# Attention block on one core: the fp32r high and low parts become fp16 pairs

## The chip, the cores and the metric

One Trainium2 chip, one core of it. The time is device microseconds (us) of one execution, the median of several; lower is better. The trace is one profiled execution. Engines: TensorE (PE, with its weight loads PEld), VectorE (DVE), ScalarE (ACT), GpSimd (POOL), SyncE (SP, which here only issues DMAs).

## The reference

Self-attention over 16 images of 32 x 32 positions (1024 tokens) with 512 channels, 8 heads of 64, all in fp32, with a residual:

```python
x = ft.reshape(B, N, C)                          # (16, 1024, 512)
qkv = x @ w_qkv + b_qkv                          # (16, 1024, 1536)
q, k, v = jnp.split(qkv.reshape(B, N, N_HEADS, 3 * D_HEAD), 3, axis=-1)
attn = jnp.einsum('bxhd,byhd->bxyh', q, k) * SCALE
attn = jax.nn.softmax(attn, axis=2)
res = jnp.einsum('bxyh,byhd->bxhd', attn, v).reshape(B, N, N_HEADS * D_HEAD)
res = res @ w_out + b_out + x
```

## The kernel before

fp32 accuracy is had from narrow matmuls: each operand is split into a high and a low part, and a product a·b is summed as hi·hi + hi·lo + lo·hi (`three_terms`). Before, x, both weights, q, k and the attention output are held as fp32r pairs (4 bytes an element); the probabilities (`p_hi`, `p_lo`) and v (`v_parts`) are fp16 pairs already.

The work is cut into 64 *steps* per image (`STEPS`), 1024 steps in all. Four steps make a *unit*: one head, 512 queries, all 1024 keys, two key tiles of 128 per step. Two units are a head, sixteen an image. In a step:

- TensorE makes the scores of the next step, for each of two key tiles one matmul with k_lo over k_hi against q_hi (L628) and one with the shift and k_hi against the row maxima and q_lo (L630), 512 columns each, into one of three PSUM banks in turn (`score_bank`);
- it makes one to three *row-max* matmuls for the next unit (L592, 512 columns, two ring banks): scores with the queries on the partitions, of which VectorE takes the maximum (L841). Once a unit the four maxima are transposed (L600) and VectorE writes them, negated, as rows of `q_shift` (L851), so that a matmul subtracts them;
- ScalarE reads each score tile twice with Exp, to fp32 (`p_full`, L740) and to fp16 (`p_hi`, L741); GpSimd (six steps in eight, L489) or VectorE (two, L860) subtracts the two into `p_lo`;
- TensorE multiplies the probabilities of the step before with v (L653 to L658): 22 fp16 matmuls of 64, 65 or 129 columns, with the probabilities stationary. The document calls these 22 the PV matmuls.

Between the two score tiles of a step stand the *fills*, work of other stages in pieces of 12 matmuls or parts of 12 (L573): the q/k projection of the next heads (`qk`, 512 columns), v (`v`, 256 columns), the output projection (`project`, 512 columns). Before a `project`, four fp32 transposes (L582) turn a token tile of the attention output. `fills_of_slot`, `ring_early`, `ring_late` and the tables above them fix by hand at which step each piece stands; every engine runs its list in order and waits on semaphores.

The parts are split as follows: ScalarE writes the high part by a copy that rounds (`x_hi` L693, `weights_hi` L698, `qk_hi` L723 and L725, `transposed_hi` L714); the low part is source minus high part, by VectorE for the weights (L785), the first image's x (L797), q and k (L824, L827) and the attention output (L808), and by GpSimd for x of later images (L483). After `qk_hi`, SP issues two DMAs inside SBUF that copy the upper half of q_hi and of k_hi to the other partitions (L427, L430).

Of the kernel before, what the change touches and what calls it, by code (L numbers as in the profile page):

```python
# [6 lines left out]
P = 128  # L7
# [6 lines left out]
PROB_BIAS = 8 * math.log(2)  # L14
QKV = 3 * DIM
# [212 lines left out]
def attention_block(nc: bass.Bass, x, xT, w_qkv, b_qkv, w_out, b_out, out):  # L228
    f32, f32r, f16 = mybir.dt.float32, mybir.dt.float32r, mybir.dt.float16
# [5 lines left out]
    with ExitStack() as ctx:  # L235
# [5 lines left out]

        wqkv_hi = sb("wqkv_hi", [P, CH_TILES, HEADS * QKV], f32r)
        wqkv_lo = sb("wqkv_lo", [P, CH_TILES, HEADS * QKV], f32r)
        wout_hi = sb("wout_hi", [P, CH_TILES, CH], f32r)
        wout_lo = sb("wout_lo", [P, CH_TILES, CH], f32r)
        xT_hi = sb("xT_hi", [P, CH_TILES, TOKENS], f32r)
        xT_lo = sb("xT_lo", [P, CH_TILES, TOKENS], f32r)
        oT_hi = sb("oT_hi", [P, O_SLOTS, CH_TILES, P], f32r)
        oT_lo = sb("oT_lo", [P, O_SLOTS, CH_TILES, P], f32r)
# [12 lines left out]
        qk_bias = sb("qk_bias", [P, HEADS], f32)  # L262
        v_bias = sb("v_bias", [P, CH_TILES], f32)
# [22 lines left out]
        consts_in = sem("consts_in")  # L286
        w_hi_done = sem("w_hi_done")
# [94 lines left out]
        def _(sp):  # L382
# [91 lines left out]
        def _(pool):  # L474
# [214 lines left out]
        def _(act):  # L689
# [20 lines left out]
            act.wait_ge(consts_in, 64)  # L710

# [5 lines left out]
            def qk_hi(b, w):  # L717
# [17 lines left out]
            def exp_tile(g, n):  # L735
                if n == 0:
# [209 lines left out]
```

## Time and profile before

| | |
|---|---|
| time, median of 3 runs | 3830.77 us (3830.4 to 3831.52) |
| span of the profiled execution | 3830.3 us |
| TensorE, matmuls | 99% of the span |
| TensorE, weight loads | 80% |
| ScalarE | 79% |
| VectorE | 71% |
| GpSimd | 52% |

The span runs from the first to the last instruction of the one profiled execution; it lies inside the range of the timed runs, so about 0.5 us stands between it and the median. A matmul's end is modelled, so TensorE's 99% is not a measure of how full it is: the distance from one matmul's start to the next one's is. On ScalarE, VectorE and GpSimd, rows that follow each other overlap at their ends a little, too.

### The profile page before, as it was taken

How to read it: one execution, taken by the hardware profiler on the slowest of the kernel's cores; microseconds unless marked ns; L12 is line 12 of the kernel's file. 1: busy time of each engine (PE TensorE's matmuls, PEld its weight loads, DVE VectorE, ACT ScalarE, POOL GpSimd, SP SyncE). 2: the span in 40 equal slices, each digit the busy share in tenths (PEclk: the TensorE clock that was granted, in tenths of full speed). 3: DMA queues.
4: the chain of work that ended last, by engine and by line, in shares of the span. 5: the costliest groups of instructions: out<-in, count | busy, mean ns of one | idle time of the engine just before them, and what ended most of it. 6: DMA issues, size and time to landing. Idle time of an engine off the chain costs nothing.

```text
span 3830.3 us, 93450 instructions
## 1 busy us (share of the span) xinstructions
PE 3776.0 (99%) x37132; PEld 3081.0 (80%) x37132; DVE 2715.5 (71%) x4643; ACT 3044.9 (79%) x5141; POOL 1983.5 (52%) x1022
## 2 busy tenths in 40 slices
PE   7999999999999999999999999999999999999998
PEld 5878888887888888888888888878888788888886
DVE  6777767777676776777767677776776767767775
ACT  5887878878787887878878788787887878878786
POOL 2464644556445464454645546455454544646444
PEclk9999999999999999999999999999999999999999
DMA  3011111212102121021211211112011111111111
GB/s 94 21 54 45 54 47 26 59 40 56 48 23 67 35 56 48 21 73 29 56 48 34 66 26 54 48 40 65 23 54 48 51 51 26 54 48 43 51 25 54
DMA packets 100709, 178.26 MB, mean 47 GB/s; under 512 B 16192, under 2 KB 16192, under 8 KB 100288
## 3 DMA queue, kind: packets, MB, share of 16 engines
q1 hardware_dynamic: 100288, 172.29, 16.2%
q8 instruction: 307, 5.03, 0.5%
q14 instruction: 114, 0.93, 0.1%
HBM read 71.57 MB, written 33.55 MB: 27 GB/s over the span
## 4 chain that ended last, share of the span: by engine, by line
PE 91%; POOL 2%; issue 2%; DVE 2%; ACT 2%; DMA 0%; SPq 0%; ACTq 0%; DVEq 0%
PE psum L573 35%; PE psum L592 13%; PE psum L628 11%; PE psum L630 11%; PE psum L653 5%; PE psum L655 5%; PE psum L654 4%; PE psum L658 3%; PE psum L657 1%; PE psum L582 1%; POOL xT_lo L483 1%; POOL p_lo L489 1%; PE psum L600 1%; ACT p_hi L741 1%; DVE max_parts L841 0%
## 5 line engine op out<-in xcount | busy, mean ns | idle before, releaser
L489 POOL TENSOR_TENSOR p_lo<-p_full,p_hi 128x1024 f16<-128x1024 f32 x768 | 1647.7, 2145 | 1681.1 <-ACT p_hi L741 1679.8
L841 DVE TENSOR_REDUCE max_parts<-psum 128x1 f32<-128x512 f32 x2048 | 1376.3, 684 | 595.2 <-PE psum L592 594.5
L740 ACT ACTIVATE p_full<-psum,prob_bias 128x512 f32<-128x512 f32 x2048 | 1425.6, 696 | 260.7 <-PE psum L630 246.4
L741 ACT ACTIVATE p_hi<-psum,prob_bias 128x512 f16<-128x512 f32 x2048 | 1422.1, 694 | 0.0
L592 PE MATMUL psum<-k_lo_hi,q_hi_hi 128*128 128x512 f32 x2048 | 854.2, 437 | 12.0 <-DMA q_hi_hi<-q_hi_hi 6.7
L628 PE MATMUL psum<-q_hi_hi,k_lo_hi 128*128 128x512 f32 x2048 | 810.3, 396 | 6.3 <-DVE q_shift L851 3.4
L630 PE MATMUL psum<-q_shift,k_shift 128*128 128x512 f32 x2048 | 805.0, 393 | 0.0
L653 PEld LDWEIGHTS psum<-v_parts,p_hi 128*128 128x128 f16 x6144 | 568.0, 98 | 280.2 <-issue 248.4
L653 PE MATMUL psum<-v_parts,p_hi 128*128 128x65 f16 x6144 | 765.1, 194 | 11.5 <-POOL p_lo L489 11.5
L654 PE MATMUL psum<-v_parts,p_hi 128*128 128x64 f16 x6144 | 756.3, 193 | 0.0
L655 PE MATMUL psum<-v_parts,p_lo 128*128 128x65 f16 x6144 | 752.6, 194 | 0.0
L655 PEld LDWEIGHTS psum<-v_parts,p_lo 128*128 128x128 f16 x6144 | 576.0, 97 | 0.0
L654 PEld LDWEIGHTS psum<-v_parts,p_hi 128*128 128x128 f16 x6144 | 575.3, 97 | 0.2
L592 PEld LDWEIGHTS psum<-k_lo_hi,q_hi_hi 128*128 128x128 f32 x2048 | 384.6, 188 | 81.8 <-issue 23.0
L658 PE MATMUL psum<-v_parts,p_hi 128*128 128x129 f16 x2048 | 447.5, 219 | 0.0
L630 PEld LDWEIGHTS psum<-q_shift,k_shift 128*128 128x128 f32 x2048 | 385.6, 188 | 72.2
L628 PEld LDWEIGHTS psum<-q_hi_hi,k_lo_hi 128*128 128x128 f32 x2048 | 387.8, 189 | 68.5 <-ACT p_hi L741 13.6
L573 PE MATMUL psum<-xT_hi,wqkv_hi 128*128 128x512 f32 x1024 | 408.1, 399 | 14.3 <-DVE xT_lo L797 14.3
L851 DVE SCALAR_TENSOR_TENSOR q_shift<-psum,identity 4x512 fp32r<-4x512 f32 x256 | 173.8, 679 | 343.5 <-PE psum L600 340.9
L573 PE MATMUL psum<-xT_lo,wqkv_hi 128*128 128x512 f32 x1024 | 402.6, 393 | 0.0
L573 PE MATMUL psum<-xT_hi,wqkv_lo 128*128 128x512 f32 x1024 | 401.3, 392 | 0.0
L657 PE MATMUL psum<-v_parts,p_lo 128*128 128x65 f16 x2048 | 393.8, 192 | 0.0
(71 smaller groups left out, 5799.6 us busy)
## 6 DMA issues: line engine op xcount, KB each, us to landing
q_hi_hi<-q_hi_hi SPq DMA_DIRECT2D x256, 128.0 KB, 2.2
k_shift<-k_lo_hi SPq DMA_DIRECT2D x256, 128.0 KB, 2.2
y_tile<-in_x SPq DMA_DIRECT2D x125, 256.0 KB, 2.7
result<-y_tile SPq DMA_DIRECT2D x125, 256.0 KB, 2.0
x_in<-in_xT SPq DMA_DIRECT2D x121, 256.0 KB, 2.9
o_heads<-in_L_conv_w_qkv SPq DMA_DIRECT2D x12, 256.0 KB, 4.5
p_full<-in_xT SPq DMA_DIRECT2D x4, 256.0 KB, 5.1
o_heads<-in_L_conv_w_out SPq DMA_DIRECT2D x4, 256.0 KB, 3.2
```

Source lines behind the costliest of these rows:

```text
L489: nc.gpsimd.tensor_tensor(p_lo[:, g % LO_SLOTS, :, :], p_full[:, g % 2, :, :], p_hi[:, g % HI_SLOTS, :, :], ALU.subtract).then_inc(p_lo_re ...
L573: matmul = nc.tensor.matmul(bank(b, w)[:, 0:width], stationary, moving, start=n == 0, stop=n == TERMS - 1)
L592: nc.tensor.matmul(bank(b, w), q_hi_hi[:, h % 2, q0:q0 + P], k_lo_hi[:, h % 2, k_half * HALF:(k_half + 1) * HALF], start=True, stop=True). ...
L628: nc.tensor.matmul(scores(g, n), k_lo_hi[:, h % 2, keys], q_hi_hi[:, h % 2, cols], start=True, stop=False)
L630: nc.tensor.matmul(scores(g, n), k_shift[:, h % 2, keys], q_shift[:, h % 2, cols], start=False, stop=True).then_inc(scores_ready, 1)
L653: nc.tensor.matmul(pv[:, qt, :], hi, v_hi, start=kt == 0 and qt == 1, stop=False, skip_group_check=True)
L654: nc.tensor.matmul(pv[:, qt, 0:DIM], hi, v_lo, start=False, stop=False, skip_group_check=True)
L655: nc.tensor.matmul(pv[:, qt, :], lo, v_hi, start=False, stop=end, skip_group_check=True)
L658: last = nc.tensor.matmul(pv_first, hi, v_all, start=False, stop=end, skip_group_check=True)
L740: nc.scalar.activation(p_full[:, g % 2, n, :], scores(g, n), ACT.Exp, scale=SCALE, bias=prob_bias[:, :])
L741: nc.scalar.activation(p_hi[:, g % HI_SLOTS, n, :], scores(g, n), ACT.Exp, scale=SCALE, bias=prob_bias[:, :]).then_inc(exp_done, 1)
L841: nc.vector.reduce_max(max_parts[:, u % 2, q_tile, k_half:k_half + 1], bank(b, w), AX.X).then_inc(done["row_max"], 1)
```

## The change

Everything held in fp32r becomes fp16: `wqkv`, `wout`, `xT`, `oT`, `k_lo_hi`, `k_shift`, `q_hi_hi`, `q_shift`. The weights are multiplied by 16 when they are split (`W_SCALE`): q and k then carry a factor of 16, which the scale of Exp takes out, and the two projections in a row one of 256, which `project_add` takes out. The row of ones that carries the shift becomes 4096 and the shift is divided by 4096. The bias of q and k is multiplied by 16 once at the start (one small ScalarE instruction, a semaphore, and one wait on ScalarE and one on VectorE, before the loop). Five VectorE lines that had one operation now have two fused in one instruction (`scalar_tensor_tensor` for `tensor_tensor`); the copies by DMA carry 2 bytes an element.

On each of the five engines the lists of instructions before and after stand in the same order, row against row, with the one added ScalarE instruction at the start as the only difference in number; the loop has the same instructions with the same waits.

The core of the diff (the same edit repeated at other tensors and places is left out):

```diff
+W_SCALE = 16.0
+SHIFT_UNIT = 4096.0
...
-        wqkv_hi = sb("wqkv_hi", [P, CH_TILES, HEADS * QKV], f32r)
+        wqkv_hi = sb("wqkv_hi", [P, CH_TILES, HEADS * QKV], f16)
...
-        xT_hi = sb("xT_hi", [P, CH_TILES, TOKENS], f32r)
+        xT_hi = sb("xT_hi", [P, CH_TILES, TOKENS], f16)
...
-        k_lo_hi = sb("k_lo_hi", [P, 2, TOKENS], f32r)
+        k_lo_hi = sb("k_lo_hi", [P, 2, TOKENS], f16)
...
-                sp.dma_start(q_hi_hi[DIM:P, h % 2, cols].bitcast(f32),
-                             q_hi_hi[0:DIM, h % 2, cols].bitcast(f32)).then_inc(q_hi_hi_ready[half], 16)
+                sp.dma_start(q_hi_hi[DIM:P, h % 2, cols],
+                             q_hi_hi[0:DIM, h % 2, cols]).then_inc(q_hi_hi_ready[half], 16)
...
-                nc.gpsimd.tensor_tensor(lo, x_stage(b, n), hi.bitcast(f32),
+                nc.gpsimd.tensor_tensor(lo, x_stage(b, n), hi,
                                         ALU.subtract).then_inc(x_lo_done, 1)
...
-                    nc.scalar.copy(weight_part(part, c)[0], stage[:, stage_slot(part, c), :]).then_inc(w_hi_done, 1)
+                    nc.scalar.activation(weight_part(part, c)[0], stage[:, stage_slot(part, c), :], ACT.Copy,
+                                         scale=W_SCALE).then_inc(w_hi_done, 1)
...
             act.wait_ge(consts_in, 64)
+            nc.scalar.activation(qk_bias_scaled[:, :], qk_bias[:, :], ACT.Copy, scale=W_SCALE).then_inc(qk_bias_ready, 1)
+            act.wait_ge(qk_bias_ready, 1)
...
-                nc.scalar.activation(p_full[:, g % 2, n, :], scores(g, n), ACT.Exp, scale=SCALE, bias=prob_bias[:, :])
+                nc.scalar.activation(p_full[:, g % 2, n, :], scores(g, n), ACT.Exp, scale=SCALE / (W_SCALE * W_SCALE), bias=prob_bias[:, :])
...
-            nc.vector.memset(k_shift[0:Q_TILES, :, :].bitcast(f32), 1.0).then_inc(fixed_ready, 1)
+            nc.vector.memset(k_shift[0:Q_TILES, :, :], SHIFT_UNIT).then_inc(fixed_ready, 1)
...
-                    nc.vector.tensor_tensor(lo, stage[:, stage_slot(part, c), :], hi.bitcast(f32), ALU.subtract).then_inc(w_lo_done, 1)
+                    nc.vector.scalar_tensor_tensor(lo, stage[:, stage_slot(part, c), :], W_SCALE, hi, ALU.mult,
+                                                   ALU.subtract).then_inc(w_lo_done, 1)
...
-                nc.vector.tensor_tensor(y, bank(b, w), y, ALU.add).then_inc(done["project"], 1)
+                nc.vector.scalar_tensor_tensor(y, bank(b, w), 1 / (W_SCALE * W_SCALE), y, ALU.mult,
+                                               ALU.add).then_inc(done["project"], 1)
```

## Rows read from the trace of the kernel before

**Rows 1.** The page: busy time by engine; the core's span and clock; the chain's shares.
```profile
PE 3776.0 (99%) x37132; PEld 3081.0 (80%) x37132; DVE 2715.5 (71%) x4643; ACT 3044.9 (79%) x5141; POOL 1983.5 (52%) x1022
core 0: 3830.3 us, clock 0.998
PE 91%; POOL 2%; issue 2%; DVE 2%; ACT 2%; DMA 0%; SPq 0%; ACTq 0%; DVEq 0%
```

**Rows 2.** Groups by line and shape: count, then busy us, mean ns of one.
```profile
L628 PE MATMUL psum<-q_hi_hi,k_lo_hi 128*128 128x512 f32 x2048 | 810.3, 396 | 6.3 <-DVE q_shift L851 3.4 <-ACT p_hi L741 0.9
L573 PE MATMUL psum<-xT_hi,wqkv_hi 128*128 128x512 f32 x1024 | 408.1, 399 | 14.3 <-DVE xT_lo L797 14.3
L573 PE MATMUL psum<-wqkv_hi,xT_lo 128*128 128x256 f32 x1024 | 290.3, 283 | 0.0
L573 PE MATMUL psum<-wout_hi,oT_hi 128*128 128x512 f32 x512 | 206.1, 402 | 2.4 <-DVE oT_lo L808 1.6 <-DVE x_in L836 0.8
...
L653 PEld LDWEIGHTS psum<-v_parts,p_hi 128*128 128x128 f16 x6144 | 568.0, 98 | 280.2 <-issue 248.4 <-ACT p_hi L741 29.8
L628 PEld LDWEIGHTS psum<-q_hi_hi,k_lo_hi 128*128 128x128 f32 x2048 | 387.8, 189 | 68.5 <-ACT p_hi L741 13.6 <-DVE q_shift L851 11.8
```

**Rows 3.** Timeline of TensorE (start, length, what), a fill's end and a step.
```profile
1000.37 0.40 PE L573 MATMUL psum<-wout_hi,oT_lo 128*128 128x512 f32 x1
...
1003.36 0.20 PE L653 MATMUL psum<-v_parts,p_hi 128*128 128x65 f16 x1
...
1004.03 0.22 PE L658 MATMUL psum<-v_parts,p_hi 128*128 128x129 f16 x1
```

**Rows 4.** The chain that ended last in order of time: one `v` fill.
```profile
1503.17 1.43 PE psum L573 x12
```

**Rows 5.** A stretch at the start at half clock: busy by engine; timeline.
```profile
31.92:36.83 4.91, 4.91 (x25) 4.91 (x23) 0.69 (x1) 0.37 (x1) 0.00 (x0) 0.50 0.00 0
31.92 0.41 PE L573 MATMUL psum<-wqkv_hi,xT_hi 128*128 128x256 f32 x1
...
36.83 0.36 PE L573 MATMUL psum<-wqkv_hi,xT_lo 128*128 128x256 f32 x1
```

**Rows 6.** Timeline of TensorE where a PV stretch ends.
```profile
1506.29 0.22 PE L658 MATMUL psum<-v_parts,p_hi 128*128 128x129 f16 x1
1506.31 0.48 PE L592 MATMUL psum<-k_lo_hi,q_hi_hi 128*128 128x512 f32 x1
...
1506.86 0.40 PE L630 MATMUL psum<-q_shift,k_shift 128*128 128x512 f32 x1
```

**Rows 7.** One stretch: us, busy PE, PEld, DVE, ACT, POOL, clock; chain's end.
```profile
445.50:459.00 13.50, 12.86 (x132) 9.84 (x129) 10.62 (x18) 13.40 (x24) 10.07 (x6) 1.00 0.41 121
...
456.72 2.10 POOL p_lo L489
458.95 0.19 PE psum L653
```

**Rows 8.** Timelines of VectorE and TensorE where a new head's k is split.
```profile
586.01 0.76 DVE L824 SCALAR_TENSOR_TENSOR k_lo_hi<-psum,qk_bias,k_lo_hi 64x512 fp32r<-64x512 f32 x1
...
586.86 0.47 PE L592 MATMUL psum<-k_lo_hi,q_hi_hi 128*128 128x512 f32 x1
```

**Rows 9.** Timelines of VectorE and TensorE, row maxima with two in a row.
```profile
1509.36 0.69 DVE L841 TENSOR_REDUCE max_parts<-psum 128x1 f32<-128x512 f32 x1 [1.84 <-PE psum L592]
...
1509.87 0.74 PE L592 MATMUL psum<-k_lo_hi,q_hi_hi 128*128 128x512 f32 x2
1510.44 0.39 PE L628 MATMUL psum<-q_hi_hi,k_lo_hi 128*128 128x512 f32 x1
```

**Rows 10.** Groups of ScalarE and GpSimd by line and shape.
```profile
L740 ACT ACTIVATE p_full<-psum,prob_bias 128x512 f32<-128x512 f32 x2048 | 1425.6, 696 | 260.7 <-PE psum L630 246.4 <-POOL p_lo L489 3.2
L741 ACT ACTIVATE p_hi<-psum,prob_bias 128x512 f16<-128x512 f32 x2048 | 1422.1, 694 | 0.0
L489 POOL TENSOR_TENSOR p_lo<-p_full,p_hi 128x1024 f16<-128x1024 f32 x768 | 1647.7, 2145 | 1681.1 <-ACT p_hi L741 1679.8
L483 POOL TENSOR_TENSOR xT_lo<-x_in,xT_hi 128x512 fp32r<-128x512 f32 x120 | 176.5, 1481 | 71.2 <-ACT xT_hi L693 71.2
```

**Rows 11.** Who waited for whom: total us, times, longest.
```profile
PE psum L592 <- DMA q_hi_hi<-q_hi_hi: 6.7, 1, 6.7
```

More of the change, by code:

```diff
@@ L286, in attention_block @@
         consts_in = sem("consts_in")
+        qk_bias_ready = sem("qk_bias_ready")
         w_hi_done = sem("w_hi_done")
@@ L703, in value_bias_hi @@
                 for c in range(CH_TILES):
-                    nc.scalar.activation(bias_hi[:, c, :], zeros, ACT.Identity, bias=v_bias[:, c:c + 1]).then_inc(w_hi_done, 1)
+                    nc.scalar.activation(bias_hi[:, c, :], zero_tile[:, :], ACT.Identity, bias=v_bias[:, c:c + 1]).then_inc(w_hi_done, 1)
             weights_hi(0)
@@ L723, in qk_hi @@
                 nc.scalar.activation(q_hi_hi[0:DIM, h % 2, cols], bank(b, w)[0:DIM, :], ACT.Identity,
-                                     bias=qk_bias[0:DIM, h:h + 1]).then_inc(q_hi_done, 1)
+                                     bias=qk_bias_scaled[0:DIM, h:h + 1]).then_inc(q_hi_done, 1)
                 nc.scalar.activation(k_lo_hi[DIM:P, h % 2, cols], bank(b, w)[DIM:P, :], ACT.Identity,
-                                     bias=qk_bias[DIM:P, h:h + 1]).then_inc(hi_done["qk"], 1)
+                                     bias=qk_bias_scaled[DIM:P, h:h + 1]).then_inc(hi_done["qk"], 1)
             def v_hi(b, w):
@@ L739, in exp_tile @@
                 wait(act, scores_ready, KEYS_PER_STEP * g + n + 1)
-                nc.scalar.activation(p_full[:, g % 2, n, :], scores(g, n), ACT.Exp, scale=SCALE, bias=prob_bias[:, :])
+                nc.scalar.activation(p_full[:, g % 2, n, :], scores(g, n), ACT.Exp, scale=SCALE / (W_SCALE * W_SCALE), bias=prob_bias[:, :])
                 nc.scalar.activation(p_hi[:, g % HI_SLOTS, n, :], scores(g, n), ACT.Exp,
-                                     scale=SCALE, bias=prob_bias[:, :]).then_inc(exp_done, 1)
+                                     scale=SCALE / (W_SCALE * W_SCALE), bias=prob_bias[:, :]).then_inc(exp_done, 1)
             for g, batches in SLOTS:
@@ L796, in _ @@
                 hi, lo = x_part(n)
-                nc.vector.tensor_tensor(lo, x_stage(0, n), hi.bitcast(f32), ALU.subtract).then_inc(first_x_lo_done, 1)
+                nc.vector.tensor_tensor(lo, x_stage(0, n), hi, ALU.subtract).then_inc(first_x_lo_done, 1)
             weights_lo(1)
             dve.wait_ge(consts_in, 64)
+            dve.wait_ge(qk_bias_ready, 1)
             def bias_of_output():
                 dve.wait_ge(bias_product, 1)
-                nc.vector.tensor_tensor(out_bias[:, :], psum[:, PV_BANK, :], out_bias[:, :], ALU.add).then_inc(bias_ready, 1)
+                nc.vector.scalar_tensor_tensor(out_bias[:, :], psum[:, PV_BANK, :], 1 / W_SCALE, out_bias[:, :], ALU.mult,
+                                               ALU.add).then_inc(bias_ready, 1)
             def transposed_lo(b, w):
@@ L823, in qk_lo @@
                 cols = slice(half * HALF, (half + 1) * HALF)
-                nc.vector.scalar_tensor_tensor(k_lo_hi[0:DIM, h % 2, cols], src[DIM:P, :], qk_bias[DIM:P, h:h + 1],
-                                               k_lo_hi[DIM:P, h % 2, cols].bitcast(f32), ALU.add,
+                nc.vector.scalar_tensor_tensor(k_lo_hi[0:DIM, h % 2, cols], src[DIM:P, :], qk_bias_scaled[DIM:P, h:h + 1],
+                                               k_lo_hi[DIM:P, h % 2, cols], ALU.add,
                                                ALU.subtract).then_inc(k_lo_done, 1)
-                nc.vector.scalar_tensor_tensor(q_shift[DIM:P, h % 2, cols], src[0:DIM, :], qk_bias[0:DIM, h:h + 1],
-                                               q_hi_hi[0:DIM, h % 2, cols].bitcast(f32), ALU.add,
+                nc.vector.scalar_tensor_tensor(q_shift[DIM:P, h % 2, cols], src[0:DIM, :], qk_bias_scaled[0:DIM, h:h + 1],
+                                               q_hi_hi[0:DIM, h % 2, cols], ALU.add,
                                                ALU.subtract).then_inc(done["qk"], 1)
@@ L852, in shift_rows @@
                     q_shift[0:Q_TILES, h % 2, half * HALF:(half + 1) * HALF].rearrange("r (t q) -> r t q", q=P),
-                    bank(b, w)[0:Q_TILES, 0:P].rearrange("r (o q) -> r o q", o=1).broadcast_to([Q_TILES, Q_TILES, P]), -1.0,
+                    bank(b, w)[0:Q_TILES, 0:P].rearrange("r (o q) -> r o q", o=1).broadcast_to([Q_TILES, Q_TILES, P]), -1.0 / SHIFT_UNIT,
                     identity[0:Q_TILES, 0:Q_TILES].rearrange("r (t o) -> r t o", o=1).broadcast_to([Q_TILES, Q_TILES, P]),
```

37 lines of the change are left out of this document (19 added, 18 removed).

## The prediction, made before the changed kernel was run

> **What bounds the kernel now.** I read the page first: the chain of work that ended last lies on TensorE for 91% of the span, and the other engines are busy 79%, 71% and 52% [rows 1]. That matmuls are "busy" 99% says little, since their ends are modelled; so the second view is the timeline of TensorE, where I measure from start to start. Three things are to be seen there. First, the 512-column fp32r matmuls follow each other without a gap: from 1000.37 to 1003.36 there are 13 of them, 2.99 us, 230 ns each [rows 3]; the 256-column ones take 1.43 us for 12, 119.2 ns [rows 4]. Second, at full clock (2.4 GHz, granted share 0.998 [rows 1]) 512 and 256 columns at one a cycle are 213.3 and 106.7 ns: 16.7 and 12.5 ns of each matmul are not columns. At the start, where the granted share is 0.50 (1.2 GHz), 23 matmuls of 256 columns take 4.91 us, 213.5 ns each [rows 5], just 256 cycles: there the extra is hidden. Third, the fp16 matmuls of PV: from 1003.36 to 1004.03 there are 21, with 2 x 776 - 129 = 1423 columns, which are 592.9 ns; the rows give 670 ns, so 3.7 ns extra per matmul [rows 3]. The difference between the types that a row shows is the weight load: 98 ns a record for fp16, 189 ns for fp32r [rows 2]. So the kernel is bound by the rate at which TensorE takes matmuls, and the fp32r ones carry an extra that fp16 ones of the same kernel don't.
>
> **The change part by part.** No instruction of the loop is moved, added or taken away; the types change.
>
> *512-column matmuls.* L628, L630 and L592 have 2048 each, the q/k projection 3 x 1024, the output projection 3 x 512 [rows 2] (one row of each kind stands there): 10752. With the fp16 extra each takes 213.3 + 3.7 = 217.0 ns, 13.0 less: 139.8 us. No row shows a 512-column fp16 matmul. Its bounds are the column rate alone (213.3) and the present 230; I take 217.0, because it is the extra of 21 fp16 matmuls with weight loads of the same 128 x 128 shape.
>
> *256-column matmuls.* 3 x 1024 [rows 2]: 119.2 to 106.7 + 3.7 = 110.4, 8.8 less: 27.0 us.
>
> *From PV to fp32r.* From the last PV matmul at 1506.29 to 1506.86, 0.57 us pass for 129 + 512 + 512 columns [rows 6]; by the rates above they would be 57.5 + 230 + 230 = 517.5 ns. So 52.5 ns are lost there: an fp32r load behind short matmuls is not covered. That is 53 ns as 128 columns at 2.4 GHz would be. It stands in three of a unit's four steps (in the fourth the small transpose L600 stands between), 768 times: 40.3 us, gone when all is fp16. The fp32 transposes L582 keep their type; they follow 512-column matmuls, which cover their load, so I add nothing.
>
> Together 207.1 us of TensorE's time. What of it lies on the path? Three places give some back, because TensorE then arrives before something that it already only just meets.
>
> *Once an image.* Between 445.5 and 459.0 ScalarE is busy 13.40 of 13.50 us, and the stretch ends with GpSimd's p_lo at 456.72 + 2.10 and PV at 458.95 [rows 7]: four steps in which x of the next image is split and q/k of a new head are read out. There ScalarE and GpSimd set the pace. TensorE's 132 matmuls are 88 of PV and 44 others; 44 x 13 + 3 x 52.5 ns = 0.73 us are gained for nothing, 15 times: 11 us.
>
> *A new head's k.* L592 at 586.86 starts just as VectorE's L824 ends (586.01 + 0.76) [rows 8]. From the L592 before it TensorE would gain 5 matmuls and one change of type, 0.12 us, and wait instead. There are 128 heads: 15 us at most, none at least; I take 8.
>
> *Two row maxima in a row.* The second L592 starts about 1510.19 (one matmul and a bit before 1510.44), 0.14 us after the reduction that frees its bank (1509.36 + 0.69 = 1510.05) [rows 9]. That is close to a wait; what TensorE gains since the third L592 (2 x 13 + 53 = 79 ns) may be lost in each of 256 units: 0 to 20 us; I take 10.
>
> *ScalarE.* Writing fp16 costs what fp32 costs: 694 against 696 ns [rows 10]. Its 79% would become 83% of the shorter span; L740 alone now idles 260.7 us, 246.4 of them behind TensorE [rows 10], so there is room for 207 us spread over the image.
>
> *GpSimd.* L483 gets the types of L489: fp32 and fp16 in, fp16 out. Half of L489's 2145 ns would be 1073, all of it 2145, against 1481 now [rows 10]. Three stand in each of the 15 stretches: from -18 to +30 us. I take none, the present 1481 being between the two and nearer to the half.
>
> *VectorE* keeps one pass over the same elements; a fused multiply is no second pass: L824 is such an instruction and takes 0.76 us for 512 columns [rows 8] where L841 takes 0.69 [rows 9]. With 128 project_adds at 0.07 us more, beside TensorE's work, this costs nothing. *DMA*: the copies carry half the bytes; the one wait for them is 6.7 us at the start [rows 11]: 0 to 4 us less, taken as none. The added bias instruction stands before the loop, behind the same start: under 1 us.
>
> Sum: 207.1 - 11 - 8 - 10 = 178 us; 3830.3 - 178 = 3652.3, and with the 0.5 us between the span and the median 3653 us.
>
> A page bears on the first term. The Trainium skill, "TensorE: Matmul & The Clock Gate", section "Wait — 56ns, not 53.3ns?", gives a fixed 2.5 ns per warm bf16 matmul, 215.7 ns for 512 columns. By it the two matmul terms would be 154 and 31 us, and the time about 3635; [rows 3] show 3.7 ns for short fp16 matmuls, and none here is 512 wide.
>
> **The rivals.**
>
> *Half of the extra belongs to the columns.* From 256 to 512 columns the fp32r matmul grows by 110.8 ns, 0.433 ns a column, where 2.4 GHz asks for 0.417 [rows 3, 4]. If fp16 keeps these 0.016 ns, it takes 225.2 and 114.5 ns: 10752 x 4.8 + 3072 x 4.7 + 40.3 = 106 us, less 15 for the three places: 3740 us. For it: two widths, one line. Against: at half clock columns cost exactly a cycle [rows 5], and four bytes a column are a trait of fp32r.
>
> *The load is covered anyway.* Behind 512 columns a load has 213 ns, and 53 is enough. Then the extra is not the load's, and only the 768 changes of type gain: 40 - 15 = 25 us, 3805 us. For it: loads fill 80% of the span beside matmuls that fill 99% [rows 1], so most of them lie under matmuls. Against: the extra differs by type. The Trainium skill says so in the same page, section "Step-by-step: what each phase is for", where the next weights load while the present matmul runs, and in "Weight-path perf modes", where the fast load, which fp32 doesn't get, is said to win with a small free dimension; by these rules 512 columns would gain nothing. Against it stand the 230 ns of [rows 3], where 216 would be all.
>
> *fp16 columns are slower.* TensorE's fp16 stream is known here only up to 129 columns. If wide fp16 matmuls paid more per column than fp32r ones, the loop would lengthen: with rows in hundredths, 129 against 65 columns is 60 against 30 ns, 0.47 a column, and 512 columns would be 240 ns; 10752 x 10 - 40 = 67 us, 3897 us. It decides from 234 ns a matmul, where 10752 x 4 eats the 40 us. Against: 21 matmuls average 3.7 ns over the column rate [rows 3].
>
> *Nothing reaches the end*: ScalarE and VectorE take it all back, 3830 us. Against it are ScalarE's 260 us behind TensorE.
>
> **How the numbers follow.** Forecast 0.64, half at the columns 0.20, covered anyway 0.09, slower 0.04, nothing 0.03. The predicted time is the forecast's, 3653. Its own bounds: 207 us and 18 from GpSimd and 4 from the copies, less 11, give 3612; with 46 us given back at the three places and 30 on GpSimd, 3699. The range must reach into the second case: 3615 to 3750 leaves about 0.19 out. A measurement of this kernel can tell about 0.2% from no change (8 us). Faster 0.64 + 0.20 + 0.09 = 0.93, same 0.03, slower 0.04.
>
> **What would show it.** Right: runs of 512-column matmuls at 217 ns from start to start and of 256 at 110; 129 + 512 + 512 columns behind PV in 0.49 us; the once-an-image stretch still about 13.4 us with ScalarE full; weight loads of L628 at 98 ns; ScalarE about 83%. Wrong: 225 ns or 230 ns for a 512-column matmul; or 217 with TensorE idle before L592, L628 and L653 for more than 50 us in sum, and VectorE or ScalarE as what ended it; or GpSimd's L483 over 2 us.

## The result and the profile after

The changed kernel takes 3603.12 us (median of 4, 3602.55 to 3604.41); the kernel before, beside it, 3830.61. The ratio is 0.9406, 95% interval 0.9392 to 0.9419: 227.5 us faster. The prediction of 3653 had the sign right and the gain some 50 us too small; the measured time lies below its range (3615 to 3750).

The page of the kernel after, busy time by engine and the shares of the chain (as in [rows 1]):

```profile
PE 3527.6 (98%) x37132; PEld 2155.3 (60%) x37132; DVE 2689.1 (75%) x4643; ACT 3015.9 (84%) x5142; POOL 1949.6 (54%) x1022
...
PE 84%; ACT 5%; POOL 4%; issue 3%; DVE 2%; DMA 0%; SPq 0%; ACTq 0%; DVEq 0%
```

TensorE still carries the chain, for 84% where it was 91%; the busy shares of ScalarE and VectorE have risen by five and four points, to 84% and 75%. The weight loads have lost 926 us of busy time. The span is 3600.7 us, 229.6 less than before; the steps below are booked against that.

Groups by line and shape (as in [rows 2] and [rows 10]; L577, L632, L634, L747 and L487 are L573, L628, L630, L740 and L483 of before; mean ns of one stands before the second bar):

```profile
L632 PE MATMUL psum<-q_hi_hi,k_lo_hi 128*128 128x512 f16 x2048 | 777.1, 379 | 18.2 <-ACT p_hi L748 10.3 <-DVE q_shift L862 6.7
L634 PEld LDWEIGHTS psum<-q_shift,k_shift 128*128 128x128 f16 x2048 | 200.3, 98 | 199.8
L747 ACT ACTIVATE p_full<-psum,prob_bias 128x512 f32<-128x512 f32 x2048 | 1430.5, 698 | 176.8 <-PE psum L634 152.3 <-POOL p_lo L493 3.4
L487 POOL TENSOR_TENSOR xT_lo<-x_in,xT_hi 128x512 f16<-128x512 f32 x120 | 158.6, 1331 | 54.6 <-ACT xT_hi L697 54.6
```

The load of a score matmul is 98 ns, where it was 189. ScalarE's Exp is unchanged (698 ns). GpSimd's x split is 150 ns shorter on average.

Timeline of TensorE, a whole fill, the next scores and a PV stretch (as in [rows 3]), and then the end of a PV stretch (as in [rows 6]; L596 is L592 of before, L657 to L662 are PV):

```profile
939.57 0.38 PE L577 MATMUL psum<-wout_hi,oT_hi 128*128 128x512 f16 x1
...
942.80 0.19 PE L657 MATMUL psum<-v_parts,p_hi 128*128 128x65 f16 x1
...
943.47 0.22 PE L662 MATMUL psum<-v_parts,p_hi 128*128 128x129 f16 x1
...
1415.56 0.22 PE L662 MATMUL psum<-v_parts,p_hi 128*128 128x129 f16 x1
1415.61 0.38 PE L596 MATMUL psum<-k_lo_hi,q_hi_hi 128*128 128x512 f16 x1
...
1416.04 0.38 PE L634 MATMUL psum<-q_shift,k_shift 128*128 128x512 f16 x1
```

From 939.57 to 942.80 there are 15 wide matmuls: 215.3 ns each by the rows. Over all 512-column fills the starts in the two traces give 215.8 ns, where 230.1 stood before. The 21 of PV take 0.67 us, as before. From the last PV matmul to the third wide one's start 0.48 us pass (1415.56 to 1416.04), where 0.57 did [rows 6]. A `v` fill in the chain (as in [rows 4]) takes 109.2 ns a matmul where it took 119.2:

```profile
432.18 1.31 PE psum L577 x12
```

By stage (starts of TensorE's records): the first PV comes 4.5 us earlier (63.3 to 58.8), 2.0 of it because the one wait for `q_hi_hi`'s copy is 4.7 us for 6.7 [rows 11]; the first image becomes 12.8 us shorter, each of the next fourteen 14.13 (235.86 to 221.72), the last 11.7, and the tail behind the last PV 2.7. Together 229.5: the gain is spread evenly, an image at a time. About half of the tail's gain is not the change's own: before, seven wide matmuls there stand 427 ns apart at a granted clock of 0.50 (1.2 GHz), 1.4 us more than at 230, and after, the granted clock of the tail is 1.00. The view of that stretch before, as in [rows 5]:

```profile
3812.40:3815.39 2.99, 2.99 (x9) 2.32 (x7) 0.00 (x0) 0.00 (x0) 0.00 (x0) 0.50 0.00 0
```

### The profile page after: what moved, and what is told of

The parts are those of the page before. It is cut to its first block, busy times and chain, and to the rows that moved or that the text cites. A ratio compares the mean times of both kernels' runs of the same rounds, so it can differ in the third digit from the quotient of the medians.

```text
span 3600.7 us, 93452 instructions
## 1 busy us (share of the span) xinstructions
PE 3527.6 (98%) x37132; PEld 2155.3 (60%) x37132; DVE 2689.1 (75%) x4643; ACT 3015.9 (84%) x5142; POOL 1949.6 (54%) x1022
## 4 chain that ended last, share of the span: by engine, by line
PE 84%; ACT 5%; POOL 4%; issue 3%; DVE 2%; DMA 0%; SPq 0%; ACTq 0%; DVEq 0%
PE psum L577 33%; PE psum L596 11%; PE psum L632 10%; PE psum L634 10%; PE psum L659 4%; PE psum L657 4%; PE psum L658 4%; POOL p_lo L493 3%; PE psum L662 3%; ACT p_full L747 2%; ACT p_hi L748 2%; PE psum L586 2%; PE psum L661 1%; POOL xT_lo L487 1%; PE psum L604 1%
## 5 line engine op out<-in xcount | busy, mean ns | idle before, releaser
L747 ACT ACTIVATE p_full<-psum,prob_bias 128x512 f32<-128x512 f32 x2048 | 1430.5, 698 | 176.8 <-PE psum L634 152.3
L632 PE MATMUL psum<-q_hi_hi,k_lo_hi 128*128 128x512 f16 x2048 | 777.1, 379 | 18.2 <-ACT p_hi L748 10.3
L634 PE MATMUL psum<-q_shift,k_shift 128*128 128x512 f16 x2048 | 776.2, 379 | 0.0
L657 PE MATMUL psum<-v_parts,p_hi 128*128 128x65 f16 x6144 | 754.3, 192 | 12.0 <-POOL p_lo L493 12.0
L596 PE MATMUL psum<-k_lo_hi,q_hi_hi 128*128 128x512 f16 x2048 | 743.9, 380 | 16.8 <-DMA q_hi_hi<-q_hi_hi 4.7
L657 PEld LDWEIGHTS psum<-v_parts,p_hi 128*128 128x128 f16 x6144 | 585.8, 98 | 136.1 <-issue 22.8
L662 PE MATMUL psum<-v_parts,p_hi 128*128 128x129 f16 x2048 | 448.1, 219 | 0.0
L862 DVE SCALAR_TENSOR_TENSOR q_shift<-psum,identity 4x512 f16<-4x512 f32 x256 | 173.7, 679 | 315.2 <-PE psum L604 311.2
L577 PE MATMUL psum<-xT_hi,wqkv_hi 128*128 128x512 f16 x1024 | 388.8, 380 | 15.0 <-DVE xT_lo L805 15.0
L577 PE MATMUL psum<-xT_lo,wqkv_hi 128*128 128x512 f16 x1024 | 388.6, 380 | 0.0
L577 PE MATMUL psum<-xT_hi,wqkv_lo 128*128 128x512 f16 x1024 | 388.6, 380 | 0.0
L871 DVE TENSOR_TENSOR p_lo<-p_full,p_hi 128x1024 f16<-128x1024 f32 x256 | 318.2, 1243 | 37.5 <-ACT p_hi L748 33.5
L634 PEld LDWEIGHTS psum<-q_shift,k_shift 128*128 128x128 f16 x2048 | 200.3, 98 | 199.8
L596 PEld LDWEIGHTS psum<-k_lo_hi,q_hi_hi 128*128 128x128 f16 x2048 | 198.2, 97 | 186.3 <-DVE max_parts L852 76.5
```

What stands on the lines that cost most here:

```text
L577: matmul = nc.tensor.matmul(bank(b, w)[:, 0:width], stationary, moving, start=n == 0, stop=n == TERMS - 1)
L596: nc.tensor.matmul(bank(b, w), q_hi_hi[:, h % 2, q0:q0 + P], k_lo_hi[:, h % 2, k_half * HALF:(k_half + 1) * HALF], start=True, stop=True). ...
L632: nc.tensor.matmul(scores(g, n), k_lo_hi[:, h % 2, keys], q_hi_hi[:, h % 2, cols], start=True, stop=False)
L634: nc.tensor.matmul(scores(g, n), k_shift[:, h % 2, keys], q_shift[:, h % 2, cols], start=False, stop=True).then_inc(scores_ready, 1)
L657: nc.tensor.matmul(pv[:, qt, :], hi, v_hi, start=kt == 0 and qt == 1, stop=False, skip_group_check=True)
L662: last = nc.tensor.matmul(pv_first, hi, v_all, start=False, stop=end, skip_group_check=True)
```

## Experiments: do the parts add up?

Three kernels hold one part in fp16 pairs and leave the others in fp32r; the fourth is the kernel after with one part left in fp32r. All four keep the scale factors and the fused instructions of the kernel after. The types that differ, for the first three against the kernel before:

```diff
 # e1_qk_only (types against before)
-        q_hi_hi = sb("q_hi_hi", [P, 2, TOKENS], f32r)
+        q_hi_hi = sb("q_hi_hi", [P, 2, TOKENS], f16)      # also k_lo_hi, k_shift, q_shift
 # e2_xw_only (types against before)
-        xT_hi = sb("xT_hi", [P, CH_TILES, TOKENS], f32r)
+        xT_hi = sb("xT_hi", [P, CH_TILES, TOKENS], f16)   # also xT_lo, wqkv_hi, wqkv_lo
 # e3_o_only (types against before)
-        oT_hi = sb("oT_hi", [P, O_SLOTS, CH_TILES, P], f32r)
+        oT_hi = sb("oT_hi", [P, O_SLOTS, CH_TILES, P], f16)   # also oT_lo, wout_hi, wout_lo
 # e10_all_but_o (from after)
-        oT_hi = sb("oT_hi", [P, O_SLOTS, CH_TILES, P], f16)
+        oT_hi = sb("oT_hi", [P, O_SLOTS, CH_TILES, P], f32r)  # also oT_lo, wout_hi, wout_lo
```

> Only q and k (k_lo_hi, k_shift, q_hi_hi, q_shift) are fp16 pairs; x, the weights and the attention output stay fp32r. Sum of parts: 6144 matmuls of 512 columns gain 14.3 ns (230.0 to 215.7, as the changed kernel shows them) = 88 us, the 768 places behind PV 43 us, and PV's own first rows 11 us, as they now stand between fp16 matmuls: 142 us, so 3688 us. Rival (what TensorE gains is given back at the waits for VectorE and ScalarE, as the prediction had it, 29 us in all, most of it in the loop of scores and row maxima): 118 us, 3712 us. Rival (PV's 11 us hang on the fills, not on q and k): 131 us, 3699 us.

> Only x and w_qkv are fp16 pairs; q, k, w_out and the attention output stay fp32r. Sum of parts: 3072 matmuls of 512 columns at 14.3 ns = 44 us, 3072 of 256 columns at 9.9 ns = 30 us; the places behind PV keep their fp32r load; GpSimd's low part of x 0.15 us shorter, three in each of 15 stretches, 6 us: 74 to 80 us, so 3750 to 3757 us. Rival (the once-an-image stretch swallows what TensorE gains there): 64 us, 3767 us.

> Only w_out and the attention output are fp16 pairs. Sum of parts: 1536 matmuls of 512 columns at 14.3 ns = 22 us, so 3809 us. Rival (nothing of it reaches the end, the projections standing where TensorE would wait anyway): 3831 us. The three kernels with one part each should together gain what the full change gains, 227.5 us, if the parts don't share a cost; more than that if each alone is given back less.

| kernel | us | ratio to before, interval | gain, us | 14.3 and 10.0 ns a matmul would give |
|---|---|---|---|---|
| q and k only | 3709.08 | 0.9684 (0.9668 to 0.97) | 121.1 | 6144 x 14.3 + 43 + 11 = 142 |
| x and its weights only | 3772.82 | 0.985 (0.9835 to 0.9865) | 57.4 | 3072 x (14.3 + 10.0) = 75 |
| attention output only | 3812.54 | 0.9954 (0.9939 to 0.9969) | 17.7 | 1536 x 14.3 = 22 |

(14.3 is 230.1 - 215.8, 10.0 is 119.2 - 109.2; 43 and 11 us belong to PV and stand in the account below.) The three gains sum to 196.2 us, the whole change has 227.5. Each part alone falls short of its matmuls: by 21, 17 and 4 us. What each of these kernels has and neither the kernel before nor after has is fills of one type among scores of the other. In their traces such stretches number 901, 714 and 187: 23, 24 and 23 ns a stretch. That points to a price for changing between the types. In the q and k kernel there is a rival, named beforehand: TensorE's matmuls wait 55.1 us for other engines, 10 more than before, so waits can be half of its 21 us. In the other two they wait 2 to 3 us less than before. The fourth kernel was made to see the price from the other end.

> The kernel after with the output projection alone (attention output and its weights) left in fp32r. If the parts add up, it gives back what this part alone brought, 17.7 us: 3621 us. If each change between fp16 and fp32r matmuls costs TensorE time, it gives back the whole of its 1536 x 14.3 ns = 22 us and the price of entering and leaving fp32r at some 170 pieces, 40 ns a pair, 7 us more: 3630 to 3632.

It took 3627.89 us (ratio 0.947, 0.9454 to 0.9485): leaving the attention output in fp32r costs 24.8 us, not the 17.7 that it brings alone. The expectation of parts that add up falls; the 24.8 lie between the two numbers of the other theory, the bare 22 us of the matmuls and 29 with 40 ns a pair, so they point to a price and don't give its size.

The traces of the four kernels show where the price stands. Timeline of TensorE in `e10_all_but_o`, from a fill's last fp32r matmul to the scores:

```profile
941.86 0.39 PE L577 MATMUL psum<-wout_hi,oT_lo 128*128 128x512 f32 x1
942.09 0.39 PE L632 MATMUL psum<-q_hi_hi,k_lo_hi 128*128 128x512 f16 x1
942.32 0.38 PE L634 MATMUL psum<-q_shift,k_shift 128*128 128x512 f16 x1
942.53 0.38 PE L632 MATMUL psum<-q_hi_hi,k_lo_hi 128*128 128x512 f16 x1
```

The first fp16 matmul behind an fp32r one takes 0.23 us to the next start, the second 0.21. In all four kernels it averages 226.5 to 226.6 ns, where 215.8 is usual. Over the two matmuls at each change, row against row with the same places before (fp32r) and after (fp16), a stretch costs 15, 19, 21 and 16 ns, most of it on the way from fp32r to fp16. With the number of stretches this is 14, 14, 4 and 3 us, so in the first two kernels a part of the shortfall is something else.

## Experiment: what is the 13 ns of an fp32r matmul?

The prediction put the extra down to the weight load, since 98 against 189 ns is what a row shows [rows 2]. Series of 40 equal matmuls behind the last of the kernel before separate load, moving columns and type (their sums are used by nobody):

```diff
+            for n in range(40):    # 128 stationary, 512 moving columns
+                nc.tensor.matmul(room, rw[:, n % 8 * P:(n % 8 + 1) * P], rm, start=n == 0, stop=n == 39)
+            for n in range(40):    # 32 stationary columns: a shorter load
+                nc.tensor.matmul(room[0:32, :], rw[:, n % 8 * P:n % 8 * P + 32], rm, start=n == 0, stop=n == 39)
+            for n in range(40):    # 256 moving columns
+                nc.tensor.matmul(room[:, 0:256], rw[:, n % 8 * P:(n % 8 + 1) * P], rm[:, 0:256], start=n == 0, stop=n == 39)
...
```

> The kernel before with series of 40 matmuls added at the end on TensorE (24 to warm up first), results unused: fp32r with 128, 64 and 32 stationary columns and 512 moving ones; fp32r 128 stationary with 256 and 384 moving; fp16 with 128, 96 and 64 stationary and 512 moving; fp16 128 stationary with 256 moving; a mix of 8 short fp16 and 2 wide fp32r. If the extra of fp32r is its weight load, it falls from 16.7 ns at 128 stationary columns to some 8 at 64 and to 2 to 5 at 32, and fp16 with 96 or 64 columns, whose load record should look like fp32r's in pace, shows some of it too. If it belongs to the moving columns, it stays at 16 to 17 ns at 64 and 32 stationary columns, and lies between 12.5 and 16.7 at 384 moving ones. If neither, fp16 and fp32r come out alike here, at 215 to 217 ns, and the extra is made by the kernel around them.

Timeline of TensorE at the end of that kernel, a series to a row (the distance to the next row's start, over 40, is the distance of two matmuls), and two groups of its loads:

```profile
3832.59 9.23 PE L695 MATMUL psum<-q_hi_hi,k_lo_hi 128*128 128x512 f32 x40
3841.65 9.36 PE L697 MATMUL psum<-q_hi_hi,k_lo_hi 128*64 128x512 f32 x40
3850.85 9.43 PE L699 MATMUL psum<-q_hi_hi,k_lo_hi 128*32 128x512 f32 x40
3860.12 4.96 PE L701 MATMUL psum<-q_hi_hi,k_lo_hi 128*128 128x256 f32 x40
3864.92 7.12 PE L703 MATMUL psum<-q_hi_hi,k_lo_hi 128*128 128x384 f32 x40
3871.88 8.81 PE L705 MATMUL psum<-p_hi 128*128 128x512 f16 x40
3880.53 8.80 PE L707 MATMUL psum<-p_hi 128*96 128x512 f16 x40
...
L695 PEld LDWEIGHTS psum<-q_hi_hi,k_lo_hi 128*128 128x128 f32 x40 | 7.5, 188 | 1.6
...
L699 PEld LDWEIGHTS psum<-q_hi_hi,k_lo_hi 128*32 128x32 f32 x40 | 4.4, 109 | 4.9
```

| type | stationary columns | moving columns | load, ns | start to start, ns | above the column rate |
|---|---|---|---|---|---|
| fp32r | 128 | 512 | 188 | 226.7 | 13.4 |
| fp32r | 64 | 512 | 134 | 230.0 | 16.7 |
| fp32r | 32 | 512 | 109 | 231.7 | 18.4 |
| fp32r | 128 | 384 | 188 | 174.0 | 14.0 |
| fp32r | 128 | 256 | 189 | 120.1 | 13.4 |
| fp16 | 128 | 512 | 97 | 216.1 | 2.8 |
| fp16 | 96 | 512 | 123 | 215.8 | 2.5 |
| fp16 | 64 | 512 | 110 | 216.5 | 3.1 |
| fp16 | 128 | 256 | 98 | 109.4 | 2.7 |

(Averages over the 39 distances within a series. The first one to six of a series can be longer; without them fp32r pays 13.3 ns at 384 columns and fp16 2.5 in all its series.) The load falls from 188 to 109 ns and the distance does not fall with it; an fp16 load of 123 ns instead of 97 changes nothing. From 256 to 512 moving columns fp32r grows by 106.6 ns, 0.416 a column, just the column rate. So the extra follows neither the length of the load nor the moving columns: it is a price of some 13.4 ns on each fp32r matmul of 256 to 512 columns with 128 stationary ones, where fp16 pays 2.5. Each matmul here has a load of its own, so a fixed price of the fp32r load isn't told apart from one of the matmul. In the running kernel 512-column fp32r matmuls average 230.0 [rows 3] and not 226.7; fp16 has no such difference (215.8). Where the 3.3 ns come from is open. The last projections of the kernel before, with the other engines nearly idle, run at 226.7 too, but idle engines are not enough: in series A of the next section fp32r matmuls stand 228 to 236 ns apart.

## Experiment: the 53 ns behind PV

Is it the load, as the prediction had it, or the change of type that the parts pointed to? Cycles of ten matmuls, eight short and two wide, with one thing changed at a time, behind the kernel before:

```diff
+            for n in range(60):    # C: the wide pair with 32 stationary columns; B has 128
+                if n % 10 < 8:
+                    nc.tensor.matmul(room[:, 0:PV_W], hw[:, n % 4 * P:(n % 4 + 1) * P], hw[:, 0:PV_W], start=True, stop=True)
+                else:
+                    nc.tensor.matmul(room[0:32, :], rw[:, n % 8 * P:n % 8 * P + 32], rm, start=True, stop=True)
...
```

> The kernel before, with 340 matmuls on data at hand added behind its last one (their sums are used by nobody). Warm-up; A: four wide fp16 matmuls (128x512) and four wide fp32r ones in turn; B: 8 fp16 matmuls of 65 columns and 2 wide fp32r ones, ten to a cycle; C: the same with 32 stationary columns in the fp32r pair; D: 8 short and 2 wide, all fp16; E: as D with 96 stationary columns in the wide pair (a load of 123 instead of 97 ns); F: 8 short (64 columns) and 2 wide, all fp32r. By the column rate and the extras of the widths run, a cycle of B and C is 8 x 29.6 + 2 x 226.7 = 690 ns, of D and E 668, of F 774 if the 13 ns stand in short ones too. Theory 'the change of type': A is some 40 ns a pair of changes above 4 x 216 + 4 x 226.7 = 1771 ns; B and C both stand near 800 ns; D, E and F lose nothing beyond their sums. Rival 'a load that short matmuls don't cover' (the prediction's reading of the 53 ns behind PV): A shows 1771 ns; B stands near 800 and C lower by some tens of ns, since its load is shorter (108 against 188 ns); E is above D; F loses 50 ns or more a cycle.

The first and the sixth cycle of each series in the timeline of TensorE (L700: A; L705: B; L710: C; L715: D; L720: E; for F, L725, the second and the sixth):

```profile
3831.70 1.04 PE L700 MATMUL psum<-p_hi 128*128 128x512 f16 x4
...
3840.73 1.04 PE L700 MATMUL psum<-p_hi 128*128 128x512 f16 x4
...
3842.52 0.42 PE L705 MATMUL psum<-p_hi 128*128 128x65 f16 x8
...
3846.53 0.42 PE L705 MATMUL psum<-p_hi 128*128 128x65 f16 x8
...
3847.32 0.42 PE L710 MATMUL psum<-p_hi 128*128 128x65 f16 x8
...
3850.94 0.42 PE L710 MATMUL psum<-p_hi 128*128 128x65 f16 x8
...
3851.66 0.42 PE L715 MATMUL psum<-p_hi 128*128 128x65 f16 x8
...
3855.05 0.41 PE L715 MATMUL psum<-p_hi 128*128 128x65 f16 x8
...
3855.72 0.41 PE L720 MATMUL psum<-p_hi 128*128 128x65 f16 x8
...
3859.17 0.41 PE L720 MATMUL psum<-p_hi 128*128 128x65 f16 x8
...
3861.22 0.97 PE L725 MATMUL psum<-q_hi_hi,k_lo_hi 128*128 128x64 f32 x8
...
3866.65 0.97 PE L725 MATMUL psum<-q_hi_hi,k_lo_hi 128*128 128x64 f32 x8
```

| series | cycle, ns | sum of its matmuls | lost |
|---|---|---|---|
| A: 4 wide fp16, 4 wide fp32r | 1806 | 1771 | 35 |
| B: 8 short fp16, 2 wide fp32r | 802 | 690 | 112 |
| C: as B, 32 stationary columns | 724 | 700 | 24 |
| D: all fp16 | 678 | 669 | 9 |
| E: all fp16, 96 stationary columns | 690 | 669 | 21 |
| F: all fp32r, 8 x 64 columns | 1358 | 774 | 584 |

(The sums use 216.1, 226.7 and 231.7 ns for the wide ones and column rate plus 2.5 or 13.4 ns for the short.) Both theories hold a part. With a load of 109 instead of 190 ns the loss falls by 88 ns (B to C), so behind short matmuls the load is uncovered, as the prediction had it. F loses without any change of type: its short fp32r matmuls stand 112 ns apart where fp16 ones stand 29, which fits the load too, though F doesn't change the load alone. PV ends with 129 columns, which give 27 ns more cover than the 65 here, and [rows 6] show 53. The change of type is real, but smaller: 35 ns a pair among wide matmuls (A), where a load has time enough; 15 in C above D. Of the 35, the two changes themselves are some 22: with the 230 ns of the running kernel for the fp32r matmuls, which is nearer to the 228 to 236 in A, its sum is 1784. D shows one thing more: the short fp16 matmuls alone are 31 ns apart on average, some 29 and some 35, which is 3.9 above their columns, while the wide ones between them keep 215.

## Experiments: what gives time back?

The prediction took 11 us off for a stretch once an image, where ScalarE and GpSimd set the pace. Timeline of GpSimd there, in the kernel before, after, and in `e11_one_later` (told below), from the first x split to the p_lo behind the stretch:

```profile
445.79 1.29 POOL L483 TENSOR_TENSOR xT_lo<-x_in,xT_hi 128x512 fp32r<-128x512 f32 x1 [0.75 <-ACT xT_hi L693]
...
459.42 2.15 POOL L489 TENSOR_TENSOR p_lo<-p_full,p_hi 128x1024 f16<-128x1024 f32 x1 [0.61 <-ACT p_hi L741]
```
```profile
418.23 1.15 POOL L487 TENSOR_TENSOR xT_lo<-x_in,xT_hi 128x512 f16<-128x512 f32 x1 [0.21 <-ACT xT_hi L697]
...
427.59 1.16 POOL L487 TENSOR_TENSOR xT_lo<-x_in,xT_hi 128x512 f16<-128x512 f32 x1
428.70 2.13 POOL L493 TENSOR_TENSOR p_lo<-p_full,p_hi 128x1024 f16<-128x1024 f32 x1
431.81 2.13 POOL L493 TENSOR_TENSOR p_lo<-p_full,p_hi 128x1024 f16<-128x1024 f32 x1 [0.98 <-ACT p_hi L748]
```
```profile
419.30 1.15 POOL L487 TENSOR_TENSOR xT_lo<-x_in,xT_hi 128x512 f16<-128x512 f32 x1 [0.21 <-ACT xT_hi L697]
...
426.57 4.24 POOL L493 TENSOR_TENSOR p_lo<-p_full,p_hi 128x1024 f16<-128x1024 f32 x2
430.77 1.16 POOL L487 TENSOR_TENSOR xT_lo<-x_in,xT_hi 128x512 f16<-128x512 f32 x1
432.88 2.13 POOL L493 TENSOR_TENSOR p_lo<-p_full,p_hi 128x1024 f16<-128x1024 f32 x1 [0.95 <-ACT p_hi L748]
```

From the first split to the last row it is 13.63 us before and 13.58 after, and the last row waited for ScalarE both times: for ScalarE the stretch kept its length, as the prediction said. Inside it the p_lo that its chain ended with starts 10.88 us after the first split before (at 456.67 by the timeline, 456.72 by the chain of [rows 7]) and 10.47 after: three x splits take 4.24 us for 4.63.

*A longer x split.* GpSimd gets a fill of 0.52 us behind each x split of the kernel after:

```diff
+                nc.gpsimd.memset(idle_tile[:, n, :], 0.0)
```

> The changed kernel with one more GpSimd instruction behind each of the 120 low parts of x: a fill of 128 x 512 fp32 in a tile that nobody reads, some 0.3 to 0.6 us (its row will say). In the changed kernel's chain three of these low parts stand in each of 15 once-an-image stretches. If the stretch's length is GpSimd's (then the 0.14 us by which each low part became shorter are 6 us of the gain, which the prediction had at nothing), the time rises by about 3 x 15 x the length of the fill, 13 to 27 us, to 3616 to 3630 us. If ScalarE alone sets the stretch, it rises by under 3 us, 3603 to 3606 us.

3624.05 us (0.9462, 0.9449 to 0.9475): 20.9 us more, 2.67 of the eight delays an image. GpSimd has no slack here: a delay of the three splits in the stretch comes through almost whole. TensorE's rows agree: of each image's 1.38 us, 0.24 and 1.14 fall in the last two steps of the stretch, and no other step changes.

*The splits elsewhere.* Is the reverse true, is a lighter GpSimd worth time? One split goes a step later, and in a second kernel another goes a step earlier, too:

```diff
-X_SPLIT_SLOT = (-18, -17, -17, -16, -14, -13, -13, -11)
+X_SPLIT_SLOT = (-18, -17, -17, -15, -14, -13, -13, -11)   # e11_one_later
+X_SPLIT_SLOT = (-18, -18, -17, -15, -14, -13, -13, -11)   # e12_spread
```

> The kernel after; the fourth of the eight pieces of the next image's x is split one step later (slot -15 for -16). In the once-an-image stretch GpSimd stands 1.16 us for it ahead of the p_lo that the stretch ends with (427.59 + 1.16, then 428.75 + 2.10); a step later GpSimd idles 0.98 us. Theory 'GpSimd sets this stretch': up to 15 x 1.16 = 17 us are gained, 3586 us; ScalarE's last p_hi of the step ends only about 0.6 us before the x part does, so 9 to 17 us, 3586 to 3594. Rival 'ScalarE, full there, sets it as much' (as the prediction read the stretch): no change, 3603.

> As e11, and the second piece one step earlier (slot -18 for -17), where ScalarE waits 1.72 us and GpSimd 3.08 us. If GpSimd sets the stretch, its chain loses a further 1.16 us and ScalarE's 0.57 us of x_hi before it: 15 x 1.16 = 17 us below e11 at most, 3570 to 3586. If something else is next after e11's move, the same as e11.

3603.22 us (0.9409, 0.9396 to 0.9422) and 3604.96 (0.9413, 0.94 to 0.9426): no change. The rows above say why: in `e11_one_later` the p_lo before the split ends at 430.8, 11.5 us after the first split instead of 12.6, and the next one still starts at 13.58, behind ScalarE. On TensorE the wait for GpSimd is gone (0.22 us from L634 to the first PV for 0.93), but the next two steps lose the same 0.7 us: 0.28 before a row-max matmul, 0.13 and 0.29 before two L632, which ScalarE's p_hi releases. So ScalarE is late there right behind GpSimd; lengthening GpSimd's work costs at once, shortening it brings nothing. In `e12_spread` the chain in this stretch goes through VectorE's p_lo and row maxima instead.

*Buffers and who does which step.* More buffers between Exp and PV, in two sizes, and VectorE taking other steps of p_lo:

```diff
-X_SLOTS, Y_SLOTS, O_SLOTS, HI_SLOTS, LO_SLOTS = 3, 3, 3, 4, 2
+X_SLOTS, Y_SLOTS, O_SLOTS, HI_SLOTS, LO_SLOTS = 3, 3, 3, 4, 3   # e6_slots, p_full 3; e8_slots_hi: 6, 4, and p_full 3
...
-POOL_STEPS = (0, 1, 2, 4, 5, 6)
+POOL_STEPS = (0, 2, 3, 4, 5, 6)   # e7_steps
```

> The changed kernel with three buffers for p_full and three for p_lo in place of two each (fp16 leaves the room). In the changed kernel TensorE waits 62.5 us in the images' steady state (my sum of gaps over 30 ns above the usual), about 2.0 of 3.9 us an image at the steps in which ScalarE waits for GpSimd to free p_full. If these buffers are the cause, 15 to 30 us go: 3573 to 3588 us. If ScalarE's or GpSimd's own work is the cause, 0 to 5 us: 3598 to 3603 us.

> As with three buffers of p_full, and four of p_lo and six of p_hi. If more buffers go on helping, 3 to 10 us below the kernel with three and three; if p_full was the only short one, the same as that within 3 us.

> The changed kernel with VectorE making p_lo in steps 1 and 7 of eight, GpSimd in the others (before: VectorE 3 and 7). The once-an-image wait of TensorE for p_lo, 0.73 us at step 49, is then VectorE's. If that wait is GpSimd's queue of x and p_lo, 5 to 11 us go, 3592 to 3598 us; if three steps in a row on GpSimd, 2 to 6 in every eight, now bind elsewhere (five times 2.1 us in 17 us is 62%), the time is 3603 to 3630 us.

3602.62 us (0.9406, 0.9393 to 0.9419) and 3603.05 (0.9407, 0.9394 to 0.942) for the buffers: no change, so none of the waits left is one for a free buffer there. 3609.86 (0.9426, 0.9413 to 0.9439) with the other steps: 6.7 us slower. There TensorE saves 0.73 us an image at the wait for p_lo and loses 1.02 in the next step, where it waits for VectorE's row_max and k_lo. None of these runs found a kernel faster than the one after.

## Why the prediction missed its range

The account, in TensorE's time, from starts to starts of the two traces:

| term | predicted, us | measured, us |
|---|---|---|
| 512 columns, 10752 | 13.0 ns: 139.8 | 14.3 ns: 153.8 |
| 256 columns, 3072 | 8.8 ns: 27.0 | 10.0 ns: 30.7 |
| PV to wide, 768 | 52.5 ns: 40.3 | 55 ns and a little: 43 |
| PV's own matmuls | not in the sum | 11 |
| sum | 207.1 | 238.5 |
| given back | 29 | 8.9, what is left over |
| net | 178 | 229.6 |

The 8.9 is no reading but the rest of the sum. Row by row some 16 us went back, as told below, so the terms above it are some 7 us short.

**What bounds the kernel** was right: TensorE's rate, read from start to start; the other engines took back some 16 us of the gain.

**The two matmul terms** were mis-sized, by 17.7 us. The step that failed first is the choice of 3.7 ns: "the extra of 21 fp16 matmuls with weight loads of the same 128 x 128 shape". That extra is one of short matmuls (D: 3.9 ns), and wide ones pay 2.5 (215.8). It was chosen because the prediction held the load for the cause, and that cause fell: a shorter load takes nothing off a 512-column matmul. The Trainium skill, "TensorE: Matmul & The Clock Gate", section "Wait — 56ns, not 53.3ns?", has 2.5 ns and 215.7 for 512 columns. This trace agrees, with 215.8; by that figure the prediction itself had worked out 154 and 31 us.

**PV to fp32r** was right in size and, mostly, in cause (B, C and F).

**PV's own matmuls** were the second failed step, a term put at nothing without a reason, and measured 11 us: the first two short ones behind fp32r are 39 and 36 ns apart in B, 29 to 35 in D. The prediction looked at what stands behind a PV stretch and not at the stretch's first matmuls.

**The places that give back** were the third: oversized, 29 us for some 16.

- *Once an image*: ScalarE set the pace, as forecast, but TensorE did gain. The matmuls of 445.54 to 458.95 take 13.41 us before and 13.03 after (417.95 to 430.98): 0.38 us gained of the 0.8 that the terms above give, so 6 to 7 us went back in 15 stretches, not 11. The PV at the end came earlier because GpSimd's x splits became shorter; the prediction had set them at no change between -18 and +30 us, and each is 0.13 us less in the stretch. The gain stayed: each of the six steps behind gains its usual 0.22 to 0.35 us.
- *A second place* was not seen beforehand: a step at 476.4, where TensorE now waits for ScalarE's p_hi. Two steps there gain 0.08 us where the terms give 0.49, 6 us in 15 images. Timeline of TensorE after, the waits of both places:

```profile
424.13 0.39 PE L632 MATMUL psum<-q_hi_hi,k_lo_hi 128*128 128x512 f16 x1 [0.29 <-ACT p_hi L748]
430.98 0.19 PE L657 MATMUL psum<-v_parts,p_hi 128*128 128x65 f16 x1 [0.55 <-POOL p_lo L493]
477.81 0.39 PE L632 MATMUL psum<-q_hi_hi,k_lo_hi 128*128 128x512 f16 x1 [0.31 <-ACT p_hi L748]
```

- *A new head's k* gave nothing back at the place that the prediction had read. Timelines of VectorE and TensorE after (as in [rows 8]):

```profile
549.51 0.69 DVE L852 TENSOR_REDUCE max_parts<-psum 128x1 f32<-128x512 f32 x1 [0.24 <-PE psum L596]
...
550.43 0.76 DVE L834 SCALAR_TENSOR_TENSOR k_lo_hi<-psum,qk_bias_scaled,k_lo_hi 64x512 f16<-64x512 f32 x1
...
549.09 0.38 PE L596 MATMUL psum<-k_lo_hi,q_hi_hi 128*128 128x512 f16 x1
...
551.28 0.38 PE L596 MATMUL psum<-k_lo_hi,q_hi_hi 128*128 128x512 f16 x1
```

  TensorE still waits for `k_lo` (550.43 + 0.76 = 551.19), but what VectorE waited for before it is a row maximum, and this is TensorE's own L596 behind a PV stretch: it comes earlier now, and the whole chain moves with it. From that L596 to the fill behind the second one it was 2.60 us before and is 2.41. The prediction treated VectorE's end as a fixed time.
- *Two row maxima in a row*: where 10 us were taken, the second L596 follows 228 ns after the first, 216 where there is no wait: 12 ns in 256 units, 3 us. The wait did appear, as forecast, as a row of the table of waits (us, times, longest), which has 6.5 us, 20 times before:

```profile
PEld psum L596 <- DVE max_parts L852: 76.5, 325, 1.3
```

**The range** failed by its own rule. The text kept 213.3 to 230 ns as the bounds of the first term, but took only the bounds of the small unknowns into the low end. With 213.3 the first term is 179.6 us, 40 more, and the forecast's own low bound of 3612 would have been 3572, below what was measured.

**The rivals.** *Half of the extra belongs to the columns* and *fp16 columns are slower*: from 256 to 512 columns an fp16 matmul of the running kernel grows by 106.6 ns (109.2 to 215.8), just the column rate. *The load is covered anyway* was right on the load behind wide matmuls and wrong on what follows: the extra is there without it. *Nothing reaches the end*: the waits of TensorE's matmuls in the table of waits sum to 45.1 us before and 60.7 after.

## What to carry to other kernels

Read a term's price from rows of the same shape or, where there are none, carry the whole spread of the nearest rows into the range: the price that decided here differed by 1.3 ns, and it stood 10752 times. Before putting a difference between two types down to what a row shows of it (here the load), ask whether that row lies on the path; a series that changes only that one thing settles it. A wait behind another engine is a give-back only if that engine is not itself waiting for the one that became faster.

## What the runs showed of the hardware

- An fp32r matmul costs a constant more than its columns: 13.4 ns at 256 and 512 moving columns, 13.3 at 384, where fp16 has 2.5; in the running kernel it is 12.5 at 256 and 16.7 at 512. At a granted clock of 0.50 none of it shows (213.5 ns at 256 columns [rows 5], 427 at 512). Fewer stationary columns make it longer (18.4 ns at 32), though their load is shorter.
- Going from fp16 to fp32r and back costs 15 to 21 ns at the changes in four kernels of mixed type; the first 512-column fp16 matmul behind fp32r takes 226.5 ns for 215.8. A type changed for all parts at once is worth more than the sum of its parts: 227.5 against 196.2 us.
- Short fp32r matmuls of 64 columns stand 112 ns apart in a stream, fp16 ones of 65 columns 29 to 35.
